# Regions of DRAM for each expert's rows, the first batch scattered by itself, experts between superblocks 4 and 5

## The reference, cut to what matters

```python
xn = layernorm(x)
s = xn @ W_spin.T + b_spin
energy = s @ W_J
affinities = softmax(energy @ s.T / sqrt(128))
attn = tanh(beta * (s + mean(s) @ W_global + affinities @ s))
logits = xn @ Wg.T + bg;  top2, weights = top_k(logits, 2), softmax of the two
gu = xn @ Wgu[e] + bgu[e];  gate, up = gu[..., ::2], gu[..., 1::2]
gated = (clip(up, -7, 7) + 1) * min(gate, 7) * sigmoid(1.702 * min(gate, 7))
ffn = sum over the two experts of weight * (gated @ Wd[e] + bd[e])
out = x + attn + ffn
```

## Time and profile before

| what | us |
|---|---|
| median of 3 runs (361.89 to 365.35) | 362.35 |
| the profiled execution | 362.15 |
| its span, first to last instruction | 360.4 |
| PE, DVE, ACT, POOL busy | 324.9, 309.9, 256.8, 203.7 |
| exponent of step 0, 16, 32, 64, 75 begins | 36.16, 70.68, 102.94, 160.50, 180.96 |
| exponent of step 76, 127 begins | 256.17, 346.09 |
| scatters on POOL (64) | 87.19 to 172.7 |
| gathers on POOL (64) | 266.03 to 349.7 |

### The profile page before, as it was taken

How to read it: one execution, slowest core, us unless ns; L and a number is a source line. 1 busy time by engine, 2 the same in 40 slices (tenths; PEclk the granted TensorE clock), 3 DMA queues, 4 the chain that set the end, 5 groups by cost and what they waited for, 6 DMA issues and landing times.

```text
span 360.4 us, 5972 instructions
## 1 busy us (share of the span) xinstructions
PE 324.9 (90%) x1778; PEld 271.9 (75%) x1779; DVE 309.9 (86%) x630; ACT 256.8 (71%) x509; POOL 203.7 (57%) x271
## 2 busy tenths in 40 slices
PE   1878999998999999999978999999899998989980
PEld 1666788776777778888768999999788786867750
DVE  5988979999978999999769999888878999987855
ACT  2754777876699797687646988888787586578751
POOL 4276851325777777777113444534137777777760
PEclk9978999999999999999999999999999999999996
DMA  5999710000111211212222877765543354555551
GB/s 148 325 332 340 282 35 0 1 31 7 51 51 54 80 46 53 90 51 82 74 87 75 241 222 229 235 207 178 178 117 107 104 164 123 131 145 133 133 126 34
DMA packets 41359, 45.97 MB, mean 128 GB/s; under 512 B 3770, under 2 KB 33082, under 8 KB 41330
## 3 DMA queue, kind: packets, MB, share of 16 engines
q1 hardware_dynamic: 36162, 32.94, 29.1%
q0 software_dynamic: 5168, 12.67, 12.4%
HBM read 23.46 MB, written 22.12 MB: 126 GB/s over the span
## 4 chain that ended last, share of the span: by engine, by line
PE 40%; DVE 22%; POOL 19%; issue 8%; ACT 5%; DMA 4%; POOLq 0%; SPq 0%; ACTq 0%; DVEq 0%
POOL made L547 9%; POOL gy L547 8%; PE PS L556 8%; PE PS L558 8%; PE PS L557 8%; DVE mx L1121 6%; DVE pl L1106 5%; PE PS L609 4%; PE PS L661 2%; PE PS L786 2%; PE PS L771 2%; DVE stats L1077 2%; DMA xy<-slots_x 1%; PE PS L788 1%; PE PS L791 1%
## 5 line engine op out<-in xcount | busy, mean ns | idle before, releaser
L921 ACT ACTIVATE PS<-PS 128x512 f32<-128x512 f32 x128 | 74.8, 585 | 42.8 <-PE PS L558 41.2
L1106 DVE TENSOR_TENSOR pl<-PS,ph 128x512 fp32r<-128x512 f32 x128 | 87.7, 685 | 14.1 <-ACT ph L932 13.5
L1121 DVE TENSOR_REDUCE mx<-PS 128x1 f32<-128x512 f32 x128 | 84.3, 682 | 6.0 <-PE PS L609 6.0
L932 ACT ACTIVATE ph<-PS 128x512 fp32r<-128x512 f32 x128 | 76.5, 598 | 12.1 <-PE PS L558 0.8
L517 POOL DMA_INDIRECT slots_x<-xn,posu x64 | 63.0, 985 | 19.7 <-issue 17.1
L609 PE MATMUL PS<-xT,gq 128*128 128x512 f32 x128 | 49.5, 423 | 6.6 <-DVE mx L1121 6.3
L556 PE MATMUL PS<-gq,xT 128*128 128x512 f32 x128 | 52.4, 410 | 1.5 <-ACT gq L937 0.8
L556 PE MATMUL PS<-ph,rows 128*128 128x512 f32 x128 | 51.5, 402 | 1.8 <-DVE pl L1106 1.8
L558 PE MATMUL PS<-gq,xT 128*128 128x512 f32 x128 | 50.1, 391 | 0.0
L558 PE MATMUL PS<-ph,rows 128*128 128x512 f32 x128 | 50.1, 391 | 0.0
L557 PE MATMUL PS<-pl,rows 128*128 128x512 f32 x128 | 50.0, 391 | 0.0
(11 more groups left out here) (199 smaller groups left out, 682.8 us busy)
## 6 DMA issues: line engine op xcount, KB each, us to landing
slots_y<-yr SPq DMA_DIRECT2D x20, 512.0 KB, 3.1
slots_x<-xs SPq DMA_DIRECT2D x1, 5120.0 KB, 22.0
xy<-slots_x SPq DMA_DIRECT2D x20, 256.0 KB, 3.0
xn<-in_L_attn_x SPq DMA_DIRECT2D x8, 256.0 KB, 5.5
w_f<-in_L_ffn_Wgu SPq DMA_DIRECT2D x1, 2048.0 KB, 12.8
late<-in_L_ffn_Wgu SPq DMA_DIRECT2D x1, 2048.0 KB, 18.3
xs<-in_L_attn_x SPq DMA_DIRECT2D x8, 256.0 KB, 3.5
out_y<-made SPq DMA_DIRECT2D x7, 256.0 KB, 3.3
```

The source lines that it names most:

```text
L921: A(S[:, n % 3], S[:, n % 3], ACT.Exp).then_inc(exp_done, 1)
L932: A(ph[:, i % RING], S[:, n % 3], ACT.Copy).then_inc(s_hi, 1)
L1106: v.tensor_tensor(dst, S[:, n % 3], high.bitcast(F32), ALU.subtract).then_inc(s_lo, 1)
L1121: v.tensor_reduce(mx4[:, a, c:c + 1], MX[:, n % 2], AX.X, ALU.max).then_inc(mx_free, 1)
```

## The change

1. **Regions in DRAM.** `slots_x` and `slots_y` have for each expert a region of 33 tiles (REGION rows). A row's place is its expert's region plus its rank, so it no longer depends on how many rows the other experts have. Batch 0 can be given its places before batch 1 is counted. Since the four tiles of a group may lie anywhere, SP loads and stores each tile by itself, at an address that it reads with a register load from a list `tile_of`: 4 loads and 4 stores per group, where there was one of each. Only the rows behind each expert's last one (`pads`, 16 transfers) and the 16 tiles for the end of the list are cleared.
2. **Routing by batch.** Counting, ranks and places are made for batch 0 (steps 13 to 16) and for batch 1 (steps 19 to 23); POOL scatters the two choices of batch 0, 16 transfers each, then those of batch 1, and between them it makes what batch 1 still lacks.
3. **The list.** The list has first the full tiles of each expert after batch 0, then all others (`tile_list`, steps 25 to 29). Groups 0 and 1 are loaded when batch 0 is scattered, and 2 and 3 after them; from group 4 on batch 1 must be scattered too.
4. **The weight** travels in a column of its own (row of 129), so the write of ones falls away. `xy` and `xs` are one buffer, so loads of x (`tokens_in`) take turns with the groups.
5. **Experts between superblocks 4 and 5** (MOE_AT = 64), without a partial sum `oT_part`. The sums in the tail come every 7 steps instead of 6, and `add_parts` goes from DVE to POOL.

```diff
-    MOE_AT = 5 * TB - 4
+    MOE_AT = 4 * TB
...
+    ETILES = NT + 1
+    REGION = ETILES * P
+    ROWS = (NE * ETILES + NE) * P
...
-    slots_x = nc.dram_tensor("slots_x", [NSLOT_TILES * P, D], F32, kind="Internal").ap()
-    slots_y = nc.dram_tensor("slots_y", [NSLOT_TILES * P, 2 * D], F32, kind="Internal").ap()
+    slots_x = nc.dram_tensor("slots_x", [ROWS, D + 1], F32, kind="Internal").ap()
+
+    slots_y = nc.dram_tensor("slots_y", [ROWS, 2 * D], U32, kind="Internal").ap()
...
-        xs = sb("xs", [P, 2, 4, D])
-        oT, oT_part = sb("oT", [P, 512]), sb("oT_part", [P, 512])
...
+        xs = sb("xs", [P, 2, 4, D + 1])
+        xy = xs
+        oT = sb("oT", [P, 512])
...
-        GLOBAL_AT = {12: 0, 14: 1}
-        COUNT_AT = {16: 0, 17: 1}
+        GLOBAL_AT = {16: 0, 28: 1}
+        COUNT_AT = {13: 0, 19: 1}
...
-        WEIGHT_LO_AT = {**{28 + n: (n,) for n in range(4)}, **{40 + n: (n,) for n in range(4, 8)},
+        WEIGHT_LO_AT = {30: (0,), 31: (1,), 37: (2,), 41: (3,), **{40 + n: (n,) for n in range(4, 8)},
```

SP:

```diff
+                def rows_at(which):
+                    _, rows = nc.values_load_multi_w_load_instructions(
+                        which, engines=(mybir.EngineType.SP,), min_val=0, max_val=ROWS - P,
+                        skip_runtime_bounds_check_because="the chip's own list of tiles")
+                    return rows
...
+                sp.wait_ge(pads_ready, 1)
+                for n in range(0, NE, 4):
+                    for row in rows_at(pad_i[0:1, n:n + 4]):
+                        sp.dma_start(slots_x[bass.ds(row, P)], zer[:]).then_inc(pads, 16)
...
-                for s in scat[0]:
-                    sp.wait_ge(s, 16 * NT // 4)
...
-                sp.wait_ge(s_fill, s_no["X", CB * TB - 1] + 1)
...
+                def group_in(g):
+                    for a, row in enumerate(rows_at(tile_of[:, 1, 4 * g:4 * g + 4])):
+                        sp.dma_start(xy[:, g % 2, a], slots_x[bass.ds(row, P)]).then_inc(xg_in[g % 2], 16)
+
+                def rows_in(g):
                     sp.wait_ge(t_fill, rows_fill(g) + 1)
-                    sp.dma_start(xy[:, u], slots_x_v[:, bass.ds(4 * g + 8, 4)]).then_inc(xg_in[u], 16)
...
+                    sp.wait_ge(w_kept, g + 1)
+                    group_in(g + 2)
...
+                def results_out(g):
+                    u, n = g % 2, g - 2
+                    rows = rows_at(tile_of[:, 1, 4 * n:4 * n + 4])
...
-                        sp.wait_ge(y_ready, 2 * g - 2)
-                    sp.dma_start(slots_y_v[:, bass.ds(4 * g - 8, 4)], yr[:, u]).then_inc(y_out[u], 16)
...
+                        sp.wait_ge(y_ready, 2 * n + 2)
+                    for a, row in enumerate(rows):
+                        sp.dma_start(slots_y[bass.ds(row, P)], yr[:, u, a].bitcast(U32)).then_inc(y_out[u], 16)
...
+                for s in scat[0]:
+                    sp.wait_ge(s, (128, 128, 256)[scat[0].index(s)])
+                sp.wait_ge(x_added, 2)
+                group_in(0)
+                group_in(1)
+                rows_in(0)
+                rows_in(1)
...
+                for s in scat[1]:
+                    sp.wait_ge(s, (128, 128, 256)[scat[1].index(s)])
+                rows_in(2)
+                rows_in(3)
+                for g in range(2, NG + 2):
+                    if g + 2 <= NG - 3:
+                        rows_in(g + 2)
...
+                    results_out(g)
                     if g < NG:
                         bias_in(g, g % 2)
```

POOL:

```diff
+            def ranks_of(b):
+                pool.wait_ge(e_free, e_no["R", b] + 1)
+                g.tensor_tensor(KEY[:, of(b)], OH1[:, of(b)], RANK[:, of(b)], ALU.mult).then_inc(route_pool, 1)
+                g.tensor_tensor(PROD[:, of(b)], OH2[:, of(b)], RANK[:, of(b)], ALU.mult).then_inc(route_pool, 1)
+
+            key_times(0, 0)
+            key_times(0, 1)
+            share_one(0)
+            choices(0)
+            share_two(0)
+            key_times(1, 0)
+            key_times(1, 1)
+            ranks_of(0)
+            choices(1)
...
-                pool.wait_ge(w_kept, n + 1)
-                g.memset(xy[:, u, :, 0], 1.0).then_inc(ones_in, 1)
...
+                    pool.wait_ge(routed, 2 * b + c + 1)
+                    pool.wait_ge(share, 3 * b + 3)
+                    for q in range(2):
+                        n = 4 * b + 2 * c + q
...
+                        if c:
+                            pool.wait_ge(scat[b][q], 128)
+                        part = slice(b * TB + 8 * q, b * TB + 8 * q + 8)
+                        g.tensor_copy(xn[:, part, D], w12[:, c, part]).then_inc(weights_in, 1)
+                        pool.wait_ge(weights_in, n + 1)
+                        for t in range(part.start, part.stop):
+                            pool.indirect_dma_start(slots_x, bass.IndirectOffsetOnAxis(ap=posu[:, c, t:t + 1], axis=0),
+                                                    xn[:, t], None).then_inc(scat[b][2 if c else q], 16)
+                        if n == 0:
+                            list_consts()
+                            share_one(1)
+                            share_two(1)
+                        if n == 1:
+                            ranks_of(1)
+                        if n == 3:
+                            pool.wait_ge(eid_ready, 1)
+                            pool.wait_ge(bd_kept, 16)
+                            pool.indirect_dma_start(b_rows[:].rearrange("t s n -> t (s n)").bitcast(F32), None, b_d,
+                                                    bass.IndirectOffsetOnAxis(ap=eid_u[0:NSLOT_TILES], axis=0)).then_inc(b_found, 16)
...
+            def add_parts(k):
+                pool.wait_ge(both_added, k + 1)
+                m = made[:, k % 4]
+                g.tensor_tensor(m[:, :, 0:D], m[:, :, 0:D], m[:, :, D:2 * D], ALU.add).then_inc(parts_added, 1)
...
+                if k:
+                    add_parts(k - 1)
```

DVE and PE:

```diff
-                pe.wait_ge(ones_in, count)
+                pe.wait_ge(xg_in[u], 64 * ((count - 1) // 2 + 1))
...
+            def ranks(b):
+
+
+                ex = (EX0, EX1)[b]
+                dve.wait_ge(tot_in, b + 1)
+                if b:
+                    link(v.tensor_copy(DATA[:, :, 0], EX0[:, :, TB]))
+                link(v.tensor_tensor_scan(scans[2 + b], scans[0], scans[1], 0.0, ALU.mult, ALU.add))
+                v.tensor_tensor(RANK[:, b * TB:b * TB + TB], E[:, TB * NE:2 * TB * NE].rearrange("p (t e) -> p t e", t=TB),
+                                ex[:, :, 0:TB].rearrange("p e t -> p t e"), ALU.add).then_inc(e_free, 1)
+
+            def places(b):
+                for c in range(2):
+                    dve.wait_ge(route_pool, 4 * b + 3 + c + 2 * (1 - b))
+                    v.tensor_reduce(mk[:, 6, b * TB:b * TB + TB], (KEY, PROD)[c][:, b * TB:b * TB + TB], AX.X, ALU.add).then_inc(dchain, 1)
+                    count[0] += 1
+                    dve.wait_ge(dchain, count[0])
+                    v.tensor_copy(posu[:, c, b * TB:b * TB + TB], mk[:, 6, b * TB:b * TB + TB]).then_inc(routed, 1)
+                    dve.wait_ge(routed, 2 * b + c + 1)
...
-            ROUTE_AT = {16: 4, 17: 5, 18: 6, 19: 7, 20: 8, 22: 9, 23: 10, 24: 11, 25: 12}
+            SHARE_AT = {13: 0, 22: 1}
+            RANKS_AT = {15: 0, 21: 1}
+            PLACES_AT = {16: 0, 23: 1}
+            LIST_AT = {25: 0, 26: 1, 28: 2, 29: 3}
...
-            BOTH_AT = {MOE_AT + 11 + 6 * k: k for k in range(7)}
-            PARTS_AT = {MOE_AT + 12 + 6 * k: k for k in range(7)}
-            FINISH_AT = {MOE_AT + 13 + 6 * k + 2 * (k == 6): k for k in range(7)}
+            BOTH_AT = {MOE_AT + 11 + 7 * k: k for k in range(7)}
+            FINISH_AT = {MOE_AT + 18 + 7 * k: k for k in range(6)}
+            FINISH_AT[126] = 6
```

371 lines of the change are left out of this document (171 added, 200 removed).

## The result

The changed kernel takes 403.53 us (median of 4 runs, 402.25 to 406.33), the kernel before 363.55 (4 runs, the three known at the prediction among them): a ratio of 1.111, 95% interval 1.102 to 1.120. I had said 395, range 377 to 408; the measured time is 0.5 us above the 385 to 403 that I gave my own forecast, and inside the wider range. The profiled execution is the longest of the four, 406.33 us, with a span of 404.6 against 360.4 of before.

A forecast was written before the change was run, and what follows sets the result against it. The prediction took POOL's gathers to set the tail and PE and DVE everything ahead of it. Its terms, 13 + 1 + 1.5 + 24 − 4.3 − 2.5 + 1.5 − 1.5 + 0.3 = +33, gave 395 us, range 377 to 408.

The forecast's parts named there:

- The hold: Routing, steps 22 and 23: DVE waits for POOL's second-batch work queued behind the scatters; +13 us, bounds 11 to 15.
- the clock: PE's granted clock falls to 1.2 GHz after it stands about 9 us in the routing; +1.5 us, between 0 and 3.4.
- SP in the expert stage: Nine transfers and two register loads per group take SP 5.5 us against 3.5; +24 us, bounds +7 to +31.
- rival 2: Expert stage: SP keeps up altogether and a group stays 3.5 us, time 371 us; chance 0.05.
- The edge of the superblock: Moving the expert stage to a superblock's edge saves a copy and eight small products: inside the rounding.
- later gathers: After the experts: the last group's result stores are four issues, so gathers begin 1.7 us later; +1.5 us (0 to 3).
- The additions on POOL: Superblocks after the experts: seven additions of 0.69 us go from DVE to POOL; −2.5 us.
- The tail: End of the kernel: gathers finish about 9 us before the last step, so the last combination begins earlier; −4.3 us.
- Rival 4: Expert stage: the second batch's last scatters land late, groups 4 and 5 wait, +5, 400 us; chance 0.08.
- rival 1: Expert stage: SP is cheaper than its spans, a group 4.1 us, the term +7, time 378 us; chance 0.12.
- rival 5: A DMA's span doesn't hold its queue, so routing wait, clock loss and SP's extra time go: 357.5 us; chance 0.04.
- rival 3: Expert stage: PE, waiting 2 us in each group, drops to 1.2 GHz and becomes the bound; 407 to 413 us; chance 0.08.

The follow-up runs named there:

- experiment 2: Changed kernel with DVE's second-batch reciprocal in step 24 instead of 22 and place numbers in step 31 instead of 23, POOL's order untouched: 395.63 us, ratio 1.090.
- experiment 1: Changed kernel with POOL's list constants and the second batch's rank products and shares put ahead of the first scatter: 401.97 us, ratio 1.105.
- experiment 3: Changed kernel with SP keeping a group's four row numbers, so one register load per group instead of two: 400.81 us, ratio 1.099.
- experiment 4: Changed kernel with a group's rows loaded by one transfer from fixed cleared tiles, without register load; experts' rows not read: 379.52 us, ratio 1.043.
- experiment 5: Kernel before with each group's rows loaded by four one-tile transfers instead of one, and results stored by four: 386.43 us, ratio 1.066.
- experiment 6: Changed kernel with later place numbers and shares, addresses loaded once per group, and two of four result stores issued by ACT: 378.22 us, ratio 1.046.
- experiment 8: Changed kernel with later place numbers and shares, and a group's rows by one transfer from cleared tiles: 370.29 us, ratio 1.019; first chip 432.34, 0.928.
- experiment 7: Two edits of the kernel before: without the last four gathers 359.24 us, ratio 0.990; part additions of six superblocks on POOL 367.10 us, ratio 1.013.
- experiment 9: Kernel before with the last superblock's parts and x added while DVE waits, last rows added in halves: 362.27 against 362.95 us, ratio 0.997.

## Why the prediction was right, and where it was off

- **The hold (+13), the list (+1), the clock (+1.5).** Right in mechanism and place, and nearly in size. That step 32 is late by the 15.5 that the three terms add up to is partly luck. In detail, the first wait is 1.41 where I had 3, the second 10.29 where I had 10, the growth ahead of step 16 is 0.5 where I had 1.0. DVE's step 24 is 13.2 us later behind step 0 (104.78 against 88.43, less 3.1), as forecast; I had not carried the 2 us or so by which PE and DVE fill up again behind the hold. With the hold gone (experiment 2) steps 0 to 32 are 14.3 us shorter, where I had 12 for the hold and 1.5 for the clock; the 1.2 that are left stand against 2.0 for the growth and the list. Experiments 1 and 2 show the cause from both sides.
- **The clock** did fall in the hold, as it had in the earlier trace rows. Window of the changed kernel from 92 us on:

```profile
92.00:105.00 13.00, 2.32 (x11) 1.68 (x11) 2.54 (x7) 2.44 (x5) 10.26 (x14) 0.73 0.12 41
...
107.00:109.00 2.00, 2.00 (x6) 1.52 (x6) 1.97 (x7) 0.00 (x0) 1.68 (x2) 0.50 0.20 66
```

  PE is busy for 2.3 of 13 us and the mean granted clock is 0.73. It is still at the lower level (0.50) when PE works again; in experiment 2, without the hold, windows of 2 us between 86 and 106 us all show 1.00. What that cost was not taken apart from the hold.
- **SP in the expert stage (+24).** The step held: 5.48 us per group against 5.5, shown by experiments 3 to 6. Its parts offset each other: a pair of issue and gap is 0.49, not 0.59, a register load 0.32, not 0.2, and the rest is the gap of 0.75 between bias and loads. The term was too small: PE's transposes of groups 6 and 19 stand 72.9 us apart, 13 groups of 5.61, against 45.8 before: +27.1. I had one group too few, and some rounds take 5.7 to 6.7 us; in those that I looked at four transfers take longer (2.35 us at 216.37 in place of 1.92).
- The Trainium skill (DMA: Bandwidth & Descriptors, Issuing engines are not separate DMA queues), by which the issue time is usually small beside the DMA, was cited for rival 2. The rows agree with its wording, 0.40 us of issue against a median of 3.0 us from issue to landing for a group's rows in the kernel before. What decides against rival 2 is the number of issues in a round: in experiment 5 six more per group, with the same bytes, cost 23 us. The floor of about 600 ns that the Trainium skill gives for a register load (same page, Latency and other measured facts) is more than what holds the queue here: experiment 3 gives 0.32 for four registers.
- **The edge of the superblock (0).** This step failed: I put the moved stage "inside the rounding", a saving too small to count, and it costs. The time from the last group's transposes to step 76, less 12 steps of attention, is 4.0 us longer than before, of which 2.9 stand between steps 64 and 68 (11.3 us against 8.4 for 76 to 80). In return steps 76 to 80, where the kernel before restarts, take 7.1 us instead of 8.4, so 2.7 are left. The rows in experiment 8 show the maxima in the way; that was not tried by moving them, so this cause is argued, not shown.
- **No wait for the ones (−1.5), later gathers (+1.5).** Groups 0 to 6 take 19.7 us against 20.9, so −1.2, but that holds a late group 5 (+1.1) too and was not taken apart. The gathers begin 2.1 us later behind the last group's transposes (22.3 us against 20.3); it costs nothing that shows, since their chain no longer ends last.
- **The additions on POOL (−2.5).** This term failed too. Steps 76 to 116 are 1.4 us shorter, but 1.3 of that is the restart between 76 and 80; from step 80 to 116 the two kernels take 65.1 and 65.0 us, though DVE has five additions less there. The edit alone (experiment 7) gives 64.7, and kernels without it between 64.4 and 65.4. So time taken off DVE there did not come back.
- **The tail (−4.3).** Right: −4.2 behind step 116, and experiment 7 finds 4.1 for that wait in the kernel before. The +0.3 at the first load of x was not looked for.
- **Rival 4**, the late second batch, with 0.08: it hardly bites in the changed kernel (group 5 is 1.1 us late), because the hold delays the stage too. With the hold off the stage grows by 3.2 us, with the scatters later by 10.7. The two costs stood one behind the other.
- **Rivals 1, 2 and 5** fall with the cycle of 5.48 and the wait of 10.29, rival 3 with the clock of 0.98 in the stage.

Of the profiled execution's 406.33 − 395 = 11.3 us, 3.1 are the start, 3.1 SP's term, 2.7 the edge, 2.4 the additions, and 0.7 stands between steps 32 and 63, less the 1.5 of the gathers that did not come; the rest is under 1 us. The 8.5 us from forecast to median are these without most of the start.

## What to carry to other kernels

Before a transfer is cut into pieces, count what its queue issues per round: in this kernel each further issue of a tile was 0.49 us on SP, whether load or store, and six more per group cost 23 us where bytes and addresses stayed the same. Work moved earlier on an in-order queue pushes back what stands behind it, so look up who waits for that, and expect that a hold taken away uncovers the next late producer (14 us taken away, 3 to 11 given back). An operation moved to another engine can only be a gain if that engine's chain is not the one that ends last, and even then it was none here.

## What the runs showed of the hardware that I had not expected

- An issue takes 0.34 us in most of ACT's rows (up to 1.0) and can overlap its running copies, and the profile shows no wait of ACT that it caused: between 190 and 250 us all waits are for PE (experiment 6).
- The first run of experiments 8 and 9 was on a chip on which the kernel before takes 466.52 us (461.93 to 472.99, 17 runs). The trace there is of the kernel of experiment 9: DVE, ACT and POOL are busy about as long as in the kernel before on the usual chip (312.0, 257.1, 202.8 us), PE 340.3 us at a mean granted clock of 0.88. Its waits between 95 and 175 us ("remote" means that the profile finds no releaser on this core):

```profile
ACT PS L921 <- remote: 48.9, 4, 20.2
...
DVE mx L1121 <- remote: 35.2, 2, 18.3
```

  PE, DVE and ACT stand for most of it; POOL's scatters run on at their pace to 170 us, and the others resume at 178. They stand again for some 30 us while the gathers run. Between 95 and 170 us the profile has no packets of the queues that carry instructions, and the next come between 170 and 180, while the kernel before on the usual chip has five of them between 90 and 170 us. That the engines lacked instructions while the scatters ran is my reading; no run tested it. The ratio of experiment 8 on that chip, 0.928, says nothing of the usual one.
